# A megakernel of gated cross-attention and a mixture of experts: another order of the shared expert's sixteen iterations, and routing steps at every second point

## The reference, cut to what matters

```python
x = x + tanh(g_xattn) * attention(layernorm(x), ctx, Wq, Wk, Wv)      # 16 batches of 100 tokens, 32 heads of 16
h = layernorm(x).reshape(-1, 512)                                      # 1600 tokens
logits = h @ router_w.T                                                # 8 experts, the best one is taken
gate, e = sigmoid(max(logits)), argmax(logits)
routed = expert_e(h * gate)                                            # silu(h @ Wg) * (h @ Wu) @ Wd, F = 1024
shared = (silu(h @ Sg) * (h @ Su)) @ Sd                                # every token, F = 1024
x = x + tanh(g_ffn) * (routed + shared)
```

## Time and profile before

| | us |
|---|---|
| median of 3 runs | 969.38 |
| the runs | 964.76, 969.38, 970.51 |
| the profiled execution | 969.12 |
| its span in the profile | 967.0 |
| PE busy within the span | 939.2 (97%) |

### The profile page before, as it was taken

The page is one execution under the profiler, slowest core; times in us unless marked ns, Lnnn a source line. Parts: engine busy times, 40 slices in busy tenths (PEclk is TensorE's granted clock), DMA queues, the critical chain, the costliest instruction groups (busy, mean ns, idle before and its releaser), DMA issues. The chain is left out here.

```text
span 967.0 us, 24702 instructions
## 1 busy us (share of the span) xinstructions
PE 939.2 (97%) x10477; PEld 779.7 (81%) x10477; DVE 626.3 (65%) x1450; ACT 549.1 (57%) x839; POOL 170.3 (18%) x206
## 2 busy tenths in 40 slices
PE   5999999999999999999789999999999999999997
PEld 4777777777777777777677999999988888988886
DVE  6887665856658665776466444433577777777774
ACT  5677777677776777677532121222356666666653
POOL 1002221122113212113243200001011122113111
PEclk9999999999999999999999999999999999999999
DMA  8554644555446565447263210012387787778761
GB/s 306 125 111 94 119 75 103 127 100 105 88 104 146 135 111 106 83 86 157 81 153 104 70 44 22 23 44 72 131 250 218 225 248 228 220 236 236 228 206 56
DMA packets 175403, 129.98 MB, mean 134 GB/s; under 512 B 114610, under 2 KB 152498, under 8 KB 175288
## 3 DMA queue, kind: packets, MB, share of 16 engines
q1 hardware_dynamic: 165864, 108.60, 44.9%
q0 software_dynamic: 6544, 16.46, 5.5%
q10 hardware_dynamic: 2880, 3.29, 1.0%
HBM read 88.79 MB, written 13.56 MB: 106 GB/s over the span
## 5 line engine op out<-in xcount | busy, mean ns | idle before, releaser
L585 PE MATMUL bank<-arena_f32r 128*128 128x512 f32 (+1 forms) x1308 | 329.6, 401 | 11.9 <-DVE arena_f32r L949 10.3
L585 PEld LDWEIGHTS bank<-arena_f32r 128*128 128x128 f32 (+1 forms) x1308 | 230.8, 183 | 73.8 <-DVE arena_f32r L901 10.5
L779 ACT ACTIVATE probs<-score_banks 128x1600 f32<-128x1600 f32 x96 | 144.9, 1509 | 45.9 <-PE score_banks L604 45.3
L1693 ACT ACTIVATE hT_hi<-arena_f 128x224 fp32r<-128x224 f32 (+2 forms) x96 | 42.2, 441 | 116.6 <-DVE arena_f L1704 116.6
L1632 PE MATMUL bank<-xnT,arena_f32r 128*128 128x224 f32 (+1 forms) x720 | 103.2, 295 | 0.0
L1632 PEld LDWEIGHTS bank<-xnT,arena_f32r 128*128 128x128 f32 x720 | 97.5, 191 | 1.8 <-issue 0.7
L619 PEld LDWEIGHTS bank<-probs,values 128*17 128x17 f32 (+1 forms) x3072 | 63.6, 97 | 26.2 <-issue 23.7
L1704 DVE TENSOR_TENSOR arena_f<-bank,arena_f 128x224 f32<-128x224 f32 (+2 forms) x93 | 41.2, 443 | 65.1 <-PE bank L1632 64.7
L619 PE MATMUL bank<-probs,values 128*17 128x100 f32 (+1 forms) x3072 | 79.2, 250 | 3.3 <-issue 2.4
L1057 POOL TENSOR_TENSOR heads_out<-heads_out,inv_sum 100x256 f32<-100x256 f32 x30 | 30.3, 1010 | 208.2 <-DVE inv_sum L1020 208.2
L1594 DVE TENSOR_TENSOR arena_f32r<-arena_f,arena_f32r 128x1024 fp32r<-128x1024 f32 x43 | 52.6, 1224 | 18.5 <-ACT arena_f32r L1587 18.5
(11 more groups left out here) (274 smaller groups left out, 1781.7 us busy)
## 6 DMA issues: line engine op xcount, KB each, us to landing
arena_f<-L_ffn_w_gate_up SPq DMA_DIRECT2D x48, 512.0 KB, 4.5
arena_f<-L_ffn_w_down SPq DMA_DIRECT2D x24, 512.0 KB, 3.8
arena_f<-ctx SPq DMA_DIRECT2D x15, 722.0 KB, 4.3
w_raw<-L_ffn_w_gate_up SPq DMA_DIRECT2D x16, 512.0 KB, 4.2
w_raw<-L_ffn_w_down SPq DMA_DIRECT2D x8, 512.0 KB, 5.6
x_all<-x SPq DMA_DIRECT2D x8, 400.0 KB
x_rows<-x_all SPq DMA_DIRECT2D x4, 800.0 KB
x_all<-x_rows POOLq DMA_DIRECT2D x4, 768.0 KB, 6.3
```

The lines of the kernel that those rows point to most:

```text
L585: product = PE.matmul(bank[0:rows, :], src[:, j, 0:rows], weight, start=(m == 0), stop=(m == 11))
L779: A.activation(k.probs[n % 2][:], k.score_banks[:, :, 0:GH * k.N].rearrange("p j (r n) -> p j r n", r=GH), ACT.Exp, scale=float(HD) ** -0. ...
L1693: A.activation(k.hT[it % 2][0][:, j, 0:width], k.hidden[j][:, 0:width], ACT.Copy).then_inc(r.h_high, 1)
```

## The change

Four things are written anew. The order of the iterations is a table of (quarter, chunk): quarters 0 and 1 of chunks 0 and 1 first, then chunk 2 of both quarters, quarter 2, and chunk 3 of quarters 0 to 2 as iterations 9 to 11; the last four are quarter 3 as before. The place of the weight splits is a second table, keyed by iteration and j; those with j = 0 stand behind `h_high` and `h_low` of the iteration's first half, those with j = 1 at its end. `route_at` gives one step at each even point from 0 on: route chunk 2 at points 0 to 28, route chunk 3 at 30 to 58. The count of the experts' lists moves from iteration 7 to iteration 9. All other edits carry the table's indices into waits and widths.

```diff
+SHARED_ORDER = ((0, 0), (0, 1), (1, 0), (1, 1), (0, 2), (1, 2), (2, 0), (2, 1),
+                (2, 2), (0, 3), (1, 3), (2, 3), (3, 0), (3, 1), (3, 2), (3, 3))
+SHARED_SPLITS = {(1, 0): 3, (1, 1): 4, (2, 1): 5, (4, 1): 6, (5, 1): 7, (6, 1): 8, (10, 1): 9, (11, 0): 10,
+                 (11, 1): 11, (13, 1): 12, (14, 1): 13, (15, 1): 14}
+COUNT_IT = 9
...
 def shared_downs(k, it):
 
-    return k.tile0[-1] * (it // CT) + k.tile0[it % CT]
+    return sum(chunk_tiles(k, c) for _, c in SHARED_ORDER[:it])
...
-    if it < min(r.it0, CT) and j == 0:
+    if it < r.it0 and u == 0 and j == 0:
         weight = [t[:] for t in k.w_first[which]]
...
 def route_at(point):
 
 
-    def ahead(p):
-        return max(0, p - 5) + max(0, min(p, 10) - 5) + max(0, min(p, 18) - 14)
-
-    return [(EARLY + n // ROUTE_STEPS, n % ROUTE_STEPS) for n in range(ahead(point), ahead(point + 1))
-            if n < 2 * ROUTE_STEPS]
+    c, step = divmod(point // 2, ROUTE_STEPS)
+    return [(EARLY + c, step)] if point % 2 == 0 and EARLY + c < CT else []
...
-def shared_splits(it):
-
-    q, c = divmod(it, 4)
-    if not c:
-        return []
-    return [2 + it - max(0, q)]
...
     for it in range(16):
-        q, c = divmod(it, 4)
+        q, c = SHARED_ORDER[it]
...
-        if it == 7:
+        if it == COUNT_IT:
...
             point += 2
+            if (it, j) in SHARED_SPLITS and j == 0:
+                act_part_high(k, r, A, w, SHARED_SPLITS[it, j])
         if it:
             act_shared_out(k, A, w, it - 1, point)
-        for part in shared_splits(it):
-            act_part_high(k, r, A, w, part)
+        if (it, 1) in SHARED_SPLITS:
+            act_part_high(k, r, A, w, SHARED_SPLITS[it, 1])
...
             point += 2
+            if (it, j) in SHARED_SPLITS and j == 0:
+                dve_part_low(k, r, V, w, SHARED_SPLITS[it, j])
         if it:
             dve_shared_add(k, V, w, it - 1, point)
-        for part in shared_splits(it):
-            dve_part_low(k, r, V, w, part)
+        if (it, 1) in SHARED_SPLITS:
+            dve_part_low(k, r, V, w, SHARED_SPLITS[it, 1])
```

More of the change, by code:

```diff
@@ L1540, in shared_downs, with chunk_tiles @@
 def shared_downs(k, it):
-    return k.tile0[-1] * (it // CT) + k.tile0[it % CT]
+    return sum(chunk_tiles(k, c) for _, c in SHARED_ORDER[:it])
+def chunk_tiles(k, c):
+    return k.tile0[c + 1] - k.tile0[c]
 def wait_unit_used(k, r, w, u):
     if u < r.u0:
-        w.wait_ge(k.shared_down, shared_downs(k, 4 * u + 4))
+        w.wait_ge(k.shared_down, shared_downs(k, SHARED_ORDER.index((u, k.NCH - 1)) + 1))
     else:
@@ L1777, in pe_shared_down @@
 def pe_shared_down(k, r, PE, w, it, point):
-    c = it % 4
+    q, c = SHARED_ORDER[it]
     for j in range(4):
@@ L1781, in pe_shared_down @@
         if t < k.tile0[c + 1]:
-            user = it - 1 if k.tile0[(it - 1) % 4] + j < k.tile0[(it - 1) % 4 + 1] else it - c - 1
-            w.wait_ge(k.x2_made, shared_downs(k, user) + j + 1 if user >= 0 else 0)
+            users = [i for i in range(it) if j < chunk_tiles(k, SHARED_ORDER[i][1])]
+            w.wait_ge(k.x2_made, shared_downs(k, users[-1]) + j + 1 if users else 0)
             if it == 0:
@@ L1788, in pe_shared_down @@
                 w.wait_ge(r.mult, 3 + j // 2)
-            made = pe_down(k, r, PE, w, it, it // 4, P * j, min(P, k.T - P * t), k.bank[4 + j], True, True)
+            made = pe_down(k, r, PE, w, it, q, P * j, min(P, k.T - P * t), k.bank[4 + j], True, True)
             made.then_inc(k.shared_down, 1)
@@ L1803, in act_shared @@
             if it or j == 0:
-                act_silu(k, r, A, w, it, j, k.width[it % 4])
+                act_silu(k, r, A, w, it, j, k.width[SHARED_ORDER[it][1]])
             for chunk, step in route_at(point + 1):
@@ L1847, in dve_shared @@
             if it or j == 0:
-                dve_mult(k, r, V, w, it, j, k.width[it % 4])
+                dve_mult(k, r, V, w, it, j, k.width[SHARED_ORDER[it][1]])
             if (it, j) == (0, 0):
                 dve_mult(k, r, V, w, 0, 1, k.width[0])
-            dve_h_low(k, r, V, w, it, j, k.width[it % 4])
+            dve_h_low(k, r, V, w, it, j, k.width[SHARED_ORDER[it][1]])
             point += 2
+            if (it, j) in SHARED_SPLITS and j == 0:
+                dve_part_low(k, r, V, w, SHARED_SPLITS[it, j])
         if it:
             dve_shared_add(k, V, w, it - 1, point)
-        for part in shared_splits(it):
-            dve_part_low(k, r, V, w, part)
+        if (it, 1) in SHARED_SPLITS:
+            dve_part_low(k, r, V, w, SHARED_SPLITS[it, 1])
         if it == 14:
@@ L1873, in dve_shared_add @@
             if q:
-                w.wait_ge(k.x2_made, shared_downs(k, it - 4) + j + 1)
+                w.wait_ge(k.x2_made, shared_downs(k, SHARED_ORDER.index((q - 1, c))) + j + 1)
             else:
```

2 lines of the change are left out of this document (1 added, 1 removed).

## The result

| | before | after |
|---|---|---|
| median of the runs, us | 969.65 (4 runs) | 978.19 (976.09 to 978.96, 4 runs) |
| ratio, with its 95% interval | 1 | 1.0085 (1.0067 to 1.0103) |
| the profiled execution, us | 969.12 | 976.09 |
| its span, us | 967.0 | 974.0 |

The change made the kernel slower by 0.85%, within the 1% that was called no change (the interval reaches just over it), and 1.0 us from the predicted 977.2. The profiled execution is the fastest of the four. Run again later, with six runs, it gave 978.63 us and 1.0089 (1.0068 to 1.0110).

A forecast was written before the change was run, and what follows sets the result against it. PE, busy 97% of the span, was taken as the bound, with 4.12 us idle to win. 2.36 + 6.04 + 1.0 + 0.7 - 3.68 + 1.7 = +8.1 us on 969.12 gave 977.2 us, range 971 to 981.5.

The forecast's parts named there:

- Part A: PE ahead of T8, with T8 and T9 ahead of the up block: 2.80 us idle, so +2.36 us.
- Part B: PE ahead of T10: L8 stands on DVE behind weight part 3's low half, which needs its load: +6.04 us.
- part E: PE's granted clock: half clock for 3.4 us behind the wait ahead of T10, +1.7 us; bounds 0 and 3.4.
- Part C: PE at T11, now behind the first down tile, waits for L9 on DVE: +1.0 us.
- Part D: Later routing steps: waits ahead of T14 (0.45 us) and T15 (0.25 us), none at the others: +0.7 us.
- -3.68: Five old PE waits go: ahead of T10, the logits, the rank, a chunk 3 turn and its transpose back, in us.
- The early load: Rival: weight part 3 is in when ACT asks, the wait ahead of T10 is 2.0 us, total 971.5 us; chance 0.12.
- the dear clock: Rival: half clock lasts twice 3.4 us and weight part 4 is late by up to 1 us: 980 us; chance 0.2.
- The thin margin of part 4: DVE finishes quarter 1's up weights 0.2 us before PE wants them; costed at nothing, without it up to 1 us.
- The case of no new waits: Rival: the old waits go and T8, T10 and T11 find their banks free: 965.4 us; chance 0.04.

The follow-up runs named there:

- the mended kernel: The change with routing steps from points 4 and 36 on and the loads of parts 3 and 4 ahead of the last store: 964.92 us, 0.9949.
- the second profile: Profile from the repetition of the changed kernel, with no edit: 978.63 us, 1.0089 to the kernel before.
- The filled waits: The change with 12 and 28 matmuls of unused result laid into the waits ahead of T8 and T10: 975.38 us, 1.0066.
- part 3 split later: The change with part 3 split at the end of iteration 1 instead of behind its first half: 973.08 us, 1.0037.
- loads first: The change with the loads of parts 3 and 4 issued ahead of the store of attention's last chunk: 971.88 us, 1.0032.
- T8 and T9 alone: The kernel before with only T8 and T9 moved ahead of the up block of iteration 1, j = 0: 970.99 us, 1.0025.
- the order alone: The change's iteration order with the old dense routing steps, parts 3 and 4 both split at the end of iteration 1: 974.13 us, 1.0055.

## Why the prediction was right

- **Where the time can come from.** The idle time between `outT` and the routing's end and its sum, 4.12 us, held: the mended kernel gained about that and no more (3.3 us of it as idle time).
- **Part A**, +2.36: right. The row says 2.55 against 0.44; with the tail of the transposes, which the sum counted from start to start, 2.8. Alone it costs 2.0. In the change it adds nothing of its own, since T10 comes at the load's time in any case; the sum respected that by taking T10's time from the load.
- **Part B**, +6.04: right. T10 was 0.2 to 0.65 us later against `outT` than forecast. In the second profile the wait was 6.58; in the first 3.22, as slow blocks filled the rest, which part E had named for the case that the clock falls behind A. So the sign that was given for B, 4 to 6 us idle ahead of T10, came to the letter in neither profile; T10's time did.
- **Part C**, +1.0: 1.04 and 1.05. **Part D**, +0.7: 0.53 + 0.36 = 0.89. The **-3.68** came in full.
- **Part E**, +1.7: right in sum and too narrow in its mechanism. It treated half clock behind T10 as sure. In the second profile it stood there and cost 2.0. In the first it stood ahead of T10, where B hid all of its 3.0 us, and behind T10 it cost nothing: the term was 0 there, one of its two bounds. The filled waits show 2 to 3 us as its share of the median.
- **The rivals.** The early load was measured by moving the load: T10's wait was 1.98 us for 2.04 worked out, and the time 971.88 for 971.5; its profile, from `outT` on, has +2.5 for the +2.4 of the sum. The fit that stands beside this rival, from the Trainium skill's page "DMA: Bandwidth & Descriptors", section "Anatomy of one DMA — SWDGE (gpsimd) path", gives about 3.2 us for such a transfer. The page states it for transfers that GpSimd issues, and these are SP's. The trace with the load ahead of the store does not contradict it (in within 3.6 us), and for the transfer as the change has it, 9.1 us decides against it. Of the dear clock one half came: the clock stood at 0.50 for 6.4 and 6.6 us, nearly twice the 3.4 of the row, but part of that lay where PE waited in any case. The thin margin of part 4 did not cost anything in either profile. The case of no new waits did not occur.
- **What was luck.** The single executions of the change lie at 975.7 to 980.6 us, so a median 1.0 us from the forecast is nearer than the forecast could know. From `outT` on, the sum's +8.1 lies between the +6.8 and +9.1 of the two profiles.

Behind the prediction I was less exact. Three of my expectations (part 3 split later, loads first, T8 and T9 alone) took half clock behind T8 from one profile and made it a rule, and so two of the gains came out at about four times what I expected, and the third edit cost half of it.

## What to carry to other kernels

Before a consumer is moved forward in an in-order queue, ask when its data land, and look at the load's landing time where it stands now, with the traffic it has now: a wait that nobody sees today (part 3 landed 5 us ahead of its use) says nothing of the place 9 us earlier. Spacing steps evenly is no aim in itself. What counts for each is whether its bank is free and its input made, and that is set by its phase within the iteration. If the critical load has to come earlier, try its place in the DMA queue first: here two lines, which put it ahead of a store, gave 6.3 to 7.2 us and no engine's order changed.

## What was not expected of the hardware

The same program falls to half clock in different places. Behind the same 2.55 us of idle time the change's first profile has 0.50 for 6.4 us (487.4 to 493.8), its second 1.00, and so have the profiles with the split later, with the loads first, and with T8 and T9 early. T10's start hardly moves by it (14.4 and 14.8 us behind `outT`), because it is the idle time that shrinks: 3.22 against 6.58 us.

In attention, before all of this, PE waits for nothing that the profile shows ("issue") ahead of the last products with `values`. The wait was 2.38 us in the profile of before, 2.40 in the change's, 1.01 in its repetition, 0.26 with the order alone, and 2.70 in the one with only the routing moved; three of the twelve profiles do not have it:

```profile
474.47 0.52 PE L626 MATMUL bank<-probs,values 105*17 105x100 f32 x11 [2.70 <-issue]
```

With the half clock that follows some of them it is likely a part of why runs of one kernel lie 4 to 6 us apart (966.8 to 973.1 in 29 runs of before); no run shows how large a part. What ends the wait there was not examined.
